# State space layer of a two-layer perceiver: where three of VectorE's scans stand among its other work

## The chip, the cores and the metric

One Trainium2 chip, of which the program uses one core. The metric is the time of one execution on the device in microseconds (us), lower is better. The kernel before took 2918.82 us, the median of three runs between 2916.55 and 2922.04 us.

## What is computed

The reference is two layers over 128 sequences of 32 tokens with 256 features: cross attention, a state space layer and a quantized feed-forward network, then a second cross attention, self attention and a mixture of experts. The change touches the state space layer alone:

```python
xz = jnp.einsum('btd,ed->bte', x, W_in)
xc, z = jnp.split(xz, 2, axis=-1)
xs = silu(conv3(xc, conv_w))
x_dbl = jnp.einsum('btd,ed->bte', xs, W_x)        # dt_param (64), Bp (16), Cp (16)
dt = softplus(dt_param @ W_dt.T + b_dt) + 1e-05
A_disc = jnp.exp(-jnp.exp(A_log)[None, None] * dt[..., None])
Bx = Bp[:, :, None, :] * dt[..., None] * xs[..., None]
s = A_t * s + Bx_t                                 # over the 32 tokens, 16 states a feature
y = C * s.sum(-1) + D_param * xs
x = x + jnp.einsum('btd,ed->bte', y, W_out) * silu(z)
```

## The kernel before

The layer is the function `state_space`. The 4096 tokens are cut into 16 tiles of 256 tokens (`NST`), and a software pipeline walks them: step n of the loop `for n in STEPS` works on tile n in its scans and on its neighbours from n - 2 to n + 4 in the parts that stand before and behind them. Every engine has an order of its own, written out by hand in its own copy of this loop, and takes its instructions strictly in that order; semaphores alone tie the engines together.

A tile has eight scans, four for each half of the features. Scan s of tile n (`scan`, L1917, one instruction of 128 x 1024 elements) reads its factors `A` and its drive, which TensorE has put into `psD[s % 2]`. There are only two such buffers. TensorE's `drive(n, s)` (L1744) therefore waits until the scan two before it has ended, and runs two scans ahead of VectorE in its own order:

```python
wait(pe, scan_done, at - 1)                  # drive(n, s): scan (n, s - 2) has ended
real(drive, n + (s + 2) // SLOTS, (s + 2) % SLOTS)   # ahead(n, s)
```

VectorE's order of a step is: scans 0 and 1, `lo_uT` (the low half of the turned inputs u, L1900, which waits for ScalarE's `hi_uT`, L1847), scan 2, `lo_xn` (L1890), scan 3, `read_out` of the tile before (L1923 and L1926; it waits until TensorE's `state_sum`, L1756, has summed all states of that tile), `lo_pb` (L1894), scans 4 and 5, `count` (L166), scan 6, `aggregate` (L170), `step_size` (L1908, which waits for ScalarE's softplus), `gate` of the tile before (L1933, which waits for TensorE's `out`), scan 7.

TensorE's order of a step is: drive 2, `turn_u` (L1730), the second quarter of the state sums, drive 3, `xnT` (L1676), the third quarter, drive 4, `dbl`, the fourth quarter, drive 5, a quarter of `conv`, drive 6, `dt_c` (it waits for `lo_pb`), a quarter of `conv`, drive 7, `out` (it waits for GpSimd's `split_y`), a quarter of `conv`, drive 0 of the next tile, the last quarter of `conv`, drive 1 of the next tile, `z`, and the first quarter of the next state sum. That one writes `psS`, which `read_out`, `out` and `gate` share, and so waits for the gate:

```python
if h == 0:
    wait(pe, o_done, n)                      # state_sum(n, 0, first)
```

GpSimd's order of a step is: `halve` of the tile before (L1628, it waits for scan 7), `split_xs`, `halve` (scan 1), `ln`, `halve` (scan 3), `split_y` (the read-out's result), half of `spread_b`, `halve` (scan 5), the other half of `spread_b`, `drive` (u, from `step_size`), and `residual` (L1640), which waits for the gate. ScalarE's `decay` (L1856) fills the factors, 32 instructions a step, with the other work between them.

Of the kernel before, what the change touches and what calls it, by code (L numbers as in the profile page):

```python
# [34 lines left out]
def wait(eng, sem, value):  # L35

    if isinstance(value, int) and value <= 0:
        return
    eng.wait_ge(sem, value)
# [1480 lines left out]
def state_space(nc, d, xres, con, norm, spent):  # L1520
# [11 lines left out]
    with ExitStack() as ctx:  # L1532
# [46 lines left out]
        def real(f, n, *more):  # L1579

            if 0 <= n < NST:
                f(n, *more)

        def flat(t):
            return t[:].rearrange("p c t -> p (c t)")

        @block.sync
        def _(sync):
            sp.clear_spent(sync)
            for t, k in ((a_log, "A_log"), (b_dt, "b_dt"), (d_par, "D_param")):  # L1590
                sync.dma_start(t[:], d[pre + k]).then_inc(const_in, 16)
            sync.dma_start(own_t[:], d["m0_own_t"]).then_inc(const_in, 16)
# [288 lines left out]
        @block.vector  # L1881
        def _(dve):
            dve.wait_ge(rate_exp, 1)
            dve.tensor_scalar(rate[:], rate[:], -1.0, None, ALU.mult).then_inc(const_ready, 1)
            dve.tensor_scalar(d_par[:], d_par[:], YS, None, ALU.mult).then_inc(const_ready, 1)
            dve.wait_ge(const_ready, 2)

            def lo_xn(n):
                dve.wait_ge(xn_hi, n + 1)
                dve.tensor_tensor(flat(xnp[1]), psX[:], flat(xnp[0]), ALU.subtract).then_inc(xn_lo, 1)  # L1890

            def lo_pb(n):
                dve.wait_ge(pb_hi, n + 1)
                dve.scalar_tensor_tensor(PB[1][:], psP[0:96, 0:ST], 1.0 / WS, PB[0][:], ALU.mult, ALU.subtract)  # L1894
                dve.tensor_tensor(Bt[1][:].rearrange("p t n -> p (t n)"), psP[:, ST:ST + 2 * NS],
                                  Bt[0][:].rearrange("p t n -> p (t n)"), ALU.subtract).then_inc(pb_lo, 1)

            def lo_uT(n):
                dve.wait_ge(uT_hi, n + 1)
                dve.scalar_tensor_tensor(flat(uT[n % 2][1]), psP[:], US, flat(uT[n % 2][0]), ALU.mult, ALU.subtract)\  # L1900
                    .then_inc(uT_lo, 1)

            def step_size(n):
                dve.wait_ge(sp_relu, n + 1)
                dve.wait_ge(sp_log, n + 1)
                wait(dve, a_done, 2 * (n - 1))
                wait(dve, u_done, n - 1)
                dve.scalar_tensor_tensor(flat(dt[n % 2]), psZ[:], 1e-5, sp_a[:], ALU.add, ALU.add).then_inc(dt_done, 1)  # L1908

            def scan(n, s):  # L1910
                k, jp, at = 2 * n + s // 4, s % 4, SLOTS * n + s
                if jp == 0:
                    dve.wait_ge(a_done, k + 1)
                    wait(dve, s_mm, k - 2)
                dve.wait_ge(drive_mm, at + 1)
                states, rates = (t[k % 3][:, 2 * jp:2 * jp + 2].rearrange("p j n t -> p (j n t)") for t in (S, A))
                dve.tensor_tensor_scan(states, rates, psD[at % 2][:], 0.0, ALU.mult, ALU.add).then_inc(scan_done, 1)  # L1917

            def read_out(n):
                dve.wait_ge(s_mm, 2 * n + 2)  # L1920
                dve.wait_ge(c_done, n + 1)
                wait(dve, yp_lo, n)
                dve.tensor_tensor(psS[:], Cm[n % 4][:], psS[:], ALU.mult).then_inc(y_prod, 1)  # L1923
                dve.wait_ge(y_prod, n + 1)
                for h in range(C):
                    last = dve.scalar_tensor_tensor(y[:, h, :], xs[n % 4][:, h * ST:(h + 1) * ST], d_par[:, h:h + 1],  # L1926
                                                    psS[:, h * ST:(h + 1) * ST], ALU.mult, ALU.add)
                last.then_inc(y_done, 1)

            def gate(n):  # L1930
                dve.wait_ge(o_mm, n + 1)
                wait(dve, x_done, n)
                dve.scalar_tensor_tensor(o[:], psS[:], 1.0 / (YS * WS), zs[n % 4][:], ALU.mult, ALU.mult).then_inc(o_done, 1)  # L1933

            def count(n):
                dve.wait_ge(x_done, n + 1)
                for g in (2 * n, 2 * n + 1):
                    statistics.count(dve, g)

            def aggregate(n):  # L1940
                for g in (2 * n, 2 * n + 1):
                    statistics.aggregate(dve, g)

            for n in STEPS:
                real(scan, n, 0)
                real(scan, n, 1)
                real(lo_uT, n + 1)
                real(scan, n, 2)
                real(lo_xn, n + 3)
                real(scan, n, 3)  # L1950
                real(read_out, n - 1)
                real(lo_pb, n + 2)
                real(scan, n, 4)
                real(scan, n, 5)
                real(count, n - 2)
                real(scan, n, 6)
                real(aggregate, n - 2)
                real(step_size, n + 2)
                real(gate, n - 1)
                real(scan, n, 7)  # L1960
            count(NST - 1)
            aggregate(NST - 1)

# [1067 lines left out]
```

## Time and profile before

| what | value |
|---|---|
| median of three runs | 2918.82 us |
| the profiled execution's own time | 2914.7 us |
| its span, first to last instruction | 2912.8 us |
| TensorE, busy | 2513.5 us, 86% of the span |
| VectorE, busy | 2056.3 us, 71% |
| ScalarE, busy | 1769.7 us, 61% |
| GpSimd, busy | 1557.9 us, 53% |
| mean granted TensorE clock | 0.926 of full speed |
| scans of the state space layer | 128, from 943.9 to 1396.4 us |

A busy share says how long an engine had an instruction in work, not how long it was the one that the others waited for. Matmuls overlap and their ends are modelled, so starts are better measured than lengths: where a length of TensorE's work is wanted, the distance from one start to the next is taken. The timeline merges neighbouring instructions of one form into one row, with their number at the end (x3), and in brackets stands how long the engine was idle before the row and who ended the idle time.

### The profile page before, as it was taken

To read this page: it belongs to the slowest core of one execution; us is meant where nothing else is said; L and a number is where in the kernel's file an instruction comes from. 1 tells how busy PE (TensorE), PEld (TensorE's weight loads), DVE (VectorE), ACT (ScalarE), POOL (GpSimd) and SP (SyncE) were. 2 spreads that over 40 slices of the span, in tenths; PEclk is the share of its full clock that TensorE was granted. 3 is DMA by queue.
4 is the path that set the end of the run, shared out by engine and by line. 5 is a ranking of instruction groups with operands and counts; after the bars stand their busy time and mean duration, and the time that the engine had idled before them with its cause. 6 is when DMAs were issued, how large, how long until landed. Compare 5 with 4: busy or idle time off the path is not lost. (4 is left out here: it accounts for less than half of the span.)

```text
span 2912.8 us, 77437 instructions
## 1 busy us (share of the span) xinstructions
PE 2513.5 (86%) x30042; PEld 1986.0 (68%) x30042; DVE 2056.3 (71%) x4606; ACT 1769.7 (61%) x4139; POOL 1557.9 (53%) x1602
## 2 busy tenths in 40 slices
PE   3999999999995898988597999999995888651998
PEld 2887788887873555554255888888884666551998
DVE  4778788788773778787344777777775888662554
ACT  2777777777774867775144666666663666443443
POOL 3656566556544777775103556556552677405443
PEclk9999999999996889998698999999997999855999
DMA  4222222222200000000001121111110000156664
GB/s 136 67 67 67 67 56 56 67 67 67 67 9 21 1 1 1 1 1 1 31 1 61 60 60 59 47 60 60 47 45 18 2 2 2 36 209 218 237 237 153
DMA packets 122999, 179.42 MB, mean 62 GB/s; under 512 B 10128, under 2 KB 106064, under 8 KB 120464
## 3 DMA queue, kind: packets, MB, share of 16 engines
q1 hardware_dynamic: 117968, 159.91, 17.9%
q0 software_dynamic: 4672, 14.57, 1.4%
q8 instruction: 244, 4.00, 0.6%
q14 instruction: 115, 0.94, 0.1%
HBM read 118.99 MB, written 14.56 MB: 46 GB/s over the span
## 5 line engine op out<-in xcount | busy, mean ns | idle before, releaser
L601 ACT ACTIVATE x_prob<-x_prob,x_nm 128x257 f32<-128x257 f32 x512 | 254.5, 499 | 176.6 <-DVE x_nm L689 176.6
L1917 DVE TENSOR_TENSOR_SCAN m_s<-m_a,m_psD 128x1024 f32<-128x1024 f32 x128 | 286.2, 2269 | 2.3 <-PE m_psD L1744 2.3
L1201 DVE SCALAR_TENSOR_TENSOR x_pTl<-x_psS,x_pTh 128x1024 f16<-128x1024 f32 x128 | 156.8, 1225 | 123.8 <-ACT x_pTh L1122 123.8
L689 DVE CUSTOM_DVE_ANT_0 x_prob<-x_psS,x_masked,x_lastv 128x256 f32<-128x256 f32 x512 | 217.3, 481 | 24.5 <-PE x_psS L513 20.6
L1856 ACT ACTIVATE m_a<-m_dt,m_rate 128x248 f32<-128x248 f32 x512 | 206.8, 492 | 0.0
L908 POOL TENSOR_TENSOR x_qbdh<-x_qh,all_mask4h 128x1024 f16<-128x1024 f16 x32 | 60.6, 1893 | 239.8 <-PE x_psV L948 236.3
L1628 POOL TENSOR_TENSOR m_s<-m_s 128x1024 f32<-128x1024 f32 x64 | 150.5, 2352 | 68.0 <-DVE m_s L1917 68.0
L1135 ACT ACTIVATE x_vh<-x_psV 128x512 f16<-128x512 f32 x128 | 76.4, 597 | 161.1 <-PE x_psV L948 161.1
L898 POOL TENSOR_SCALAR x_ctxh<-x_ctx 128x512 f16<-128x512 f32 x128 | 78.8, 616 | 163.4 <-DMA x_ctx<-in_ctxT 163.4
L418 PE MATMUL x_psK<-x_ctxh,x_wkh 128*128 128x256 f16 x512 | 141.2, 276 | 27.8 <-DVE x_kl L702 23.3
L2833 ACT ACTIVATE e1t_g<-e1t_psH,e1t_bias 128x128 f32<-128x128 f32 x312 | 88.9, 368 | 114.2 <-PE e1t_psH L2781 114.2
L900 POOL TENSOR_TENSOR x_ctxl<-x_ctx,x_ctxh 128x512 f16<-128x512 f32 x128 | 149.5, 1168 | 10.7
L352 POOL TENSOR_TENSOR x_ctxl<-x_ctx,x_ctxh 128x512 f16<-128x512 f32 x128 | 148.2, 1157 | 10.7
L948 PE MATMUL x_psK<-x_ctxh,x_wkh 128*128 128x256 f16 x512 | 141.2, 276 | 3.1 <-POOL x_ctxl L900 2.3
L1116 ACT ACTIVATE x_psS<-x_psS 128x1024 f32<-128x1024 f32 x128 | 129.2, 1009 | 24.1 <-PE x_psS L1045 24.1
L418 PE MATMUL x_psK<-x_ctxh,x_wkl 128*128 128x256 f16 x512 | 141.4, 276 | 0.0
L418 PE MATMUL x_psK<-x_ctxl,x_wkh 128*128 128x256 f16 x512 | 141.4, 276 | 0.0
L948 PE MATMUL x_psV<-x_wvh,x_ctxh 128*128 128x256 f16 x512 | 141.1, 276 | 0.0
L418 PE MATMUL x_psV<-x_wvh,x_ctxh 128*128 128x256 f16 x512 | 140.0, 274 | 0.0
L948 PE MATMUL x_psK<-x_ctxl,x_wkh 128*128 128x256 f16 x512 | 140.0, 273 | 0.0
L948 PE MATMUL x_psK<-x_ctxh,x_wkl 128*128 128x256 f16 x512 | 140.0, 273 | 0.0
L418 PE MATMUL x_psV<-x_wvl,x_ctxh 128*128 128x256 f16 x512 | 140.0, 273 | 0.0
(555 smaller groups left out, 10211.2 us busy)
## 6 DMA issues: line engine op xcount, KB each, us to landing
x_ctx<-in_ctxT SPq DMA_DIRECT2D x64, 1024.0 KB, 5.8
all_xres<-e_wh SPq DMA_DIRECT2D x39, 512.0 KB
all_xres<-e_wl SPq DMA_DIRECT2D x39, 512.0 KB
x_mraw<-in_mask SPq DMA_DIRECT2D x128, 128.5 KB, 6.0
e1r_stage<-in_L_ffn_w SPq DMA_DIRECT2D x16, 1024.0 KB, 5.2
e_rows<-e1r_pad POOLq DMA_DIRECT2D x1, 5070.0 KB, 25.0
e1t_row<-e_rows SPq DMA_DIRECT2D x39, 130.0 KB
all_xres<-in_x SPq DMA_DIRECT2D x4, 1024.0 KB, 9.8
```

What stands on the lines that cost most here:

```text
L352: pool.tensor_tensor(lo[:, j], src, hi[:, j], ALU.subtract).then_inc(ctx_split, 1)
L418: last = pe.matmul(out, a, b, start=m == 0, stop=m == len(prods) - 1)
L601: last = act.activation(prob[b % NP][:, s, :], prob[b % NP][:, s, :], ACT.Exp, bias=nm[b % NP][:, s:s + 1], scale=-1.0, accum_out=sm[b // ...
L689: dve.tensor_tensor_reduce(prob[b % NP][:, s, 0:LAST], psS[:, s * LAST:(s + 1) * LAST], masked[g % 2][:, j, :], -SC, lastv[g % 2][:, j, s: ...
L900: pool.tensor_tensor(lo[:, j], src, hi[:, j], ALU.subtract).then_inc(ctx_split, 1)
L948: last = pe.matmul(out, a, b, start=m == 0, stop=m == len(prods) - 1)
L1116: act.activation(psS[c % 2][:], psS[c % 2][:], ACT.Sigmoid, scale=SC).then_inc(sig_done, 1)
L1201: dve.scalar_tensor_tensor(pT[c % 4][1][:].rearrange("p r k n -> p (r k n)"), psS[c % 2][:], PS, pT[c % 4][0][:].rearrange("p r k n -> p ( ...
L1628: pool.tensor_tensor(lower, lower, upper, ALU.add).then_inc(half_done, 1)
L1856: last = act.activation(A[k % 3][:, :, m, 1:T], dt[n % 2][:, h, :].rearrange("p (j t) -> p j t", t=T)[:, :, 1:T], ACT.Exp, scale=rate[:, h ...
L1917: dve.tensor_tensor_scan(states, rates, psD[at % 2][:], 0.0, ALU.mult, ALU.add).then_inc(scan_done, 1)
L2833: act.activation(g[c % 2][:, k, :], psH[c % 2 * 2 + k // 4][:, k % 4 * P:(k % 4 + 1) * P], ACT.Gelu_apprx_tanh, scale=1.0 / WS, bias=bias[ ...
```

## The change

Three of VectorE's eight scans move up in its order by one place or more. Scan 2 moves ahead of `lo_uT`, scan 3 ahead of `lo_xn`, scan 4 ahead of `read_out` and `lo_pb`, and scan 7 ahead of `gate`. No instruction is added or taken away, no wait is changed, and the orders of the other engines stay. Seen from the scans, `lo_uT`, `lo_xn`, `read_out`, `lo_pb` and `gate` each come one scan later.

```diff
                 real(scan, n, 0)
                 real(scan, n, 1)
+                real(scan, n, 2)
                 real(lo_uT, n + 1)
-                real(scan, n, 2)
+                real(scan, n, 3)
                 real(lo_xn, n + 3)
-                real(scan, n, 3)
+                real(scan, n, 4)
                 real(read_out, n - 1)
                 real(lo_pb, n + 2)
-                real(scan, n, 4)
                 real(scan, n, 5)
                 real(count, n - 2)
                 real(scan, n, 6)
                 real(aggregate, n - 2)
                 real(step_size, n + 2)
+                real(scan, n, 7)
                 real(gate, n - 1)
-                real(scan, n, 7)
```

## Rows read from the trace of the kernel before

**Rows 1.** Windows: length, busy PE PEld DVE ACT POOL (x), granted clock, DMA share, GB/s
```profile
973.35:1319.68 346.33, 314.94 (x2137) 201.23 (x2136) 274.78 (x248) 252.47 (x565) 259.68 (x191) 0.91 0.00 1
1319.68:1348.31 28.63, 22.89 (x127) 13.17 (x127) 22.74 (x21) 18.95 (x44) 18.95 (x14) 0.82 0.00 1
1348.31:1375.09 26.78, 20.69 (x97) 10.75 (x97) 21.21 (x17) 13.14 (x33) 13.16 (x8) 0.75 0.00 1
1375.09:1413.00 37.91, 26.10 (x117) 16.57 (x116) 20.21 (x25) 0.00 (x0) 14.72 (x10) 0.77 0.00 0
```

**Rows 2.** Waits from 973.35 to 1319.68 us: who for whom, total us, times, longest
```profile
PE m_psD L1744 <- DVE m_s L1917: 31.1, 21, 2.5
DVE m_psS L1923 <- PE m_psS L1756: 22.4, 12, 1.9
DVE m_o L1933 <- PE m_psS L1665: 22.1, 12, 3.6
```

**Rows 3.** VectorE's timeline, one step: start us, length us, instruction, [idle before <- releaser]
```profile
1120.47 0.69 DVE L1900 SCALAR_TENSOR_TENSOR m_ut1l<-m_psP,m_ut1h 128x512 f16<-128x512 f32 x1 [1.67 <-ACT m_ut1h L1847]
1121.08 2.28 DVE L1917 TENSOR_TENSOR_SCAN m_s<-m_a,m_psD 128x1024 f32<-128x1024 f32 x1
1123.54 0.69 DVE L1890 TENSOR_TENSOR m_xnl<-m_psX,m_xnh 128x512 f16<-128x512 f32 x1 [0.18 <-ACT m_xnh L1806]
1124.14 2.28 DVE L1917 TENSOR_TENSOR_SCAN m_s<-m_a,m_psD 128x1024 f32<-128x1024 f32 x1
1128.29 0.70 DVE L1923 TENSOR_TENSOR m_psS<-m_c,m_psS 128x512 f32<-128x512 f32 x1 [1.87 <-PE m_psS L1756]
...
1130.24 4.45 DVE L1917 TENSOR_TENSOR_SCAN m_s<-m_a,m_psD 128x1024 f32<-128x1024 f32 x2
...
1135.26 2.26 DVE L1917 TENSOR_TENSOR_SCAN m_s<-m_a,m_psD 128x1024 f32<-128x1024 f32 x1
...
1138.19 0.69 DVE L1908 SCALAR_TENSOR_TENSOR m_dt<-m_psZ,m_sp_a 128x512 f32<-128x512 f32 x1 [0.53 <-issue]
1141.21 0.69 DVE L1933 SCALAR_TENSOR_TENSOR m_o<-m_psS,m_zs 128x512 f32<-128x512 f32 x1 [2.33 <-PE m_psS L1665]
1141.82 6.63 DVE L1917 TENSOR_TENSOR_SCAN m_s<-m_a,m_psD 128x1024 f32<-128x1024 f32 x3
```

**Rows 4.** TensorE's timeline, same step: drives 2 to 6, a `conv`, `out`, drives 1 and 2
```profile
1118.40 0.39 PE L1744 MATMUL m_psD<-m_bd0h,m_ut0h 32*128 32x512 f16 x2
...
1121.46 0.39 PE L1744 MATMUL m_psD<-m_bd0h,m_ut0h 32*128 32x512 f16 x2
...
1124.53 0.39 PE L1744 MATMUL m_psD<-m_bd0h,m_ut0h 32*128 32x512 f16 x2
...
1128.18 0.39 PE L1744 MATMUL m_psD<-m_bd0h,m_ut0h 32*128 32x512 f16 x2
...
1128.93 0.28 PE L1665 MATMUL m_psX<-m_xnh,m_wt1h 128*128 128x256 f16 x1
...
1132.57 0.39 PE L1744 MATMUL m_psD<-m_bd0h,m_ut0h 32*128 32x512 f16 x2 [2.48 <-DVE m_s L1917]
...
1139.69 0.28 PE L1665 MATMUL m_psS<-m_wouth,m_yh 128*128 128x256 f16 x1
...
1144.15 0.39 PE L1744 MATMUL m_psD<-m_bd1h,m_ut1h 32*128 32x512 f16 x2 [0.15 <-DVE m_s L1917]
...
1148.05 0.39 PE L1744 MATMUL m_psD<-m_bd1h,m_ut1h 32*128 32x512 f16 x2
```

**Rows 5.** TensorE alone in windows of 2 us, same step: length, busy us, granted clock
```profile
1130.00:1132.00 2.00, 0.09 (x1) 1.00 0.00 0
1134.00:1136.00 2.00, 2.00 (x11) 0.50 0.03 8
```

**Rows 6.** ScalarE's timeline, same step: the last decays before softplus, and its start
```profile
1126.88 4.81 ACT L1856 ACTIVATE m_a<-m_dt,m_rate 128x248 f32<-128x248 f32 x12
1135.20 0.84 ACT L1829 ACTIVATE m_sp_a<-m_psZ,m_b_dt 128x256 f32<-128x256 f32 x2 [3.52 <-PE m_psZ L1665]
```

## The prediction

> **What bounds the kernel now.** I read the windows first, then the waits of the longest window, then the timelines of one step on VectorE, TensorE and ScalarE. The windows are cut where TensorE starts drive 2 of tiles 1, 13, 14 and 15 (the last runs to the end of the layer). The window from 973.35 to 1319.68 us holds 12 whole steps of 28.86 us each (346.33 / 12) [rows 1]. In it TensorE is busy for 314.94 us, 91% of the time, VectorE for 22.9 us a step (274.78 / 12), GpSimd for 21.6 and ScalarE for 21.0. No engine is full, so waits between them matter. TensorE's matmuls wait for VectorE's scans for 31.1 us in all, 2.6 us a step, and the longest wait is 2.5 us [rows 2]: it is one place, once a step.
>
> The timelines show the place. All times below are offsets from T, the start of drive 2 of the step at 1118.40 us; its next start, 1148.05, makes that step 29.65 us long [rows 4]. Drive 6 needs scan 4. VectorE stands idle for 1.87 us ahead of the read-out, which starts at T+9.9 when TensorE has finished the state sums, then does `read_out` and `lo_pb`, and starts scan 4 only at T+11.84 [rows 3]. TensorE is at drive 6 at T+11.7 (1132.57 less 2.48) but starts it at T+14.17 [rows 4]. So VectorE first waits for TensorE with a scan in its hands whose drive is already there, and TensorE then waits for that scan. A second price follows. The granted clock is 1.00 in the window in which TensorE stands still and 0.50 right behind it, the lower of its two levels (1.2 instead of 2.4 GHz) [rows 5]. Over the 12 steps the clock is 0.91 [rows 1], so 0.09 x 346.3 = 31 us, another 2.6 us a step, is lost to it.
>
> **The change part by part.** Nothing is added or removed; each of the eight scans, and each moved step, has the length that it has now. Only starts move. No instruction issues a DMA, and no DMA queue is passed: the DMA share of the stage is 0.00 [rows 1].
>
> Scan 2 ahead of `lo_uT`. Scan 1 ends at T+0.4 (scans 7, 0 and 1 end at 1141.82 + 6.63 = 1148.45, the next T is 1148.05 [rows 3, 4]) and `lo_uT` waits 1.67 us for ScalarE [rows 3]. A drive takes 0.75 us (1128.18 to 1128.93 [rows 4]), so scan 2 is ready at T+0.75 and fills that wait. `lo_uT` comes some 2 us later against T. Who waits for it: `dbl`, which writes the same `psP` and starts at T+6.9, behind drive 4 (T+6.13), and drive 0 of the next tile at T+18. Both have slack; cost 0.
>
> Scan 3 ahead of `lo_xn`. Drive 3 starts at T+3.06 [rows 4]. `lo_xn` slips to about T+6.2; its first reader is `conv` at T+10.5 (1128.93) [rows 4]. Cost 0.
>
> Scan 4 ahead of `read_out` and `lo_pb`. This is the part that pays. Drive 4 is done at T+6.9 (6.13 + 0.75), so scan 4 runs from T+6.95 to T+9.2. The state sums end at T+9.9 as now, so the read-out still starts there and `split_y` and `out` behind it lose nothing. Scan 4 is over 2.5 us before TensorE reaches drive 6 at T+11.7: the 2.48 us wait goes, and I take the clock's fall with it. From drive 6 to `out` TensorE took 7.12 us (1132.57 to 1139.69), nearly all of it at half clock [rows 4, 5]. It holds two drives and 21 matmuls (12 of `dt_c`, 9 of `conv`). At full clock, `out`, a `conv`, a drive and a `conv` (30 matmuls and a drive) take 4.31 us (1139.69 to 1144.00), which is (4.31 - 0.75) / 30 = 0.12 us a matmul, so the middle costs 21 x 0.12 + 2 x 0.75 = 4.0 us: 3.1 us less. What is late next: `dt_c` needs `lo_pb`, which still ends at T+11.84, before drive 6 is over at T+12.4. Drive 7 needs scan 5: from T+11.85 to T+14.1, while TensorE is there at T+14.9.
>
> Scan 7 ahead of `gate`. VectorE waits 2.33 us for `out` in this step and 22.1 us in 12 steps [rows 2, 3]. Scan 6 now runs from T+14.7 to T+16.9, and `step_size` to T+17.65 if softplus is there. ScalarE ends its decays at T+13.3 (1126.88 + 4.81) and its softplus takes 3 us (1135.20 to `step_size` at 1138.19), so T+16.3 [rows 3, 6]: in time by 0.7 us. Scan 7 runs to T+19.9. Drive 1 of the next tile, which needs it, is reached at T+20.0 (11.7, 4.0 for the middle and 4.3 from `out` on [rows 4]). These are so near to each other that I allow for a wait of 0 to 0.3 us where there were 0.15. The gate, queued behind, ends at T+20.5. Behind it on VectorE are scans 0 and 1, on GpSimd `residual` and the halving of scan 7, and on TensorE the first quarter of the state sums, which starts at most 2.3 us ahead of the next drive 2 (drives 2 and 3 are 3.06 apart, with a drive, `turn_u` and such a quarter between their starts [rows 4]), so not before T+21.7. Cover 1.2 us; cost 0.
>
> The new step: 29.65 - 2.48 - 3.1 = 24.0 (24.1 with the little wait at its longest). The mean comes out alike: 28.86 - 2.6 - 2.6 = 23.7, and the waits that stay. VectorE's 22.9 us fit into 24.0 with 1.1 to spare, so TensorE sets the pace with hardly a pause. I take 24.0. Saved: 12 x 4.85 = 58 us.
>
> Outside the 12 steps: steps 13 and 14 take 28.63 and 26.78 us with VectorE busy for 22.74 and 21.21 and the clock at 0.82 and 0.75 [rows 1]. They can't fall below VectorE's work, so they give at most 5.9 and 5.6; TensorE has less to do there and will still wait here and there, so I take 5 and 4 (bounds 2 and 5.7 each). The last window starts with a step of the same kind, but there the halving of scan 7 stands behind the `residual` that waits for the gate, so I take 1 (0 to 3). Tile 0's step has no read-out; I take 1 (0 to 2.4, the steady wait). Sum: 58 + 11 = 69 us.
>
> One rule of the Trainium skill speaks against the term for the clock. First the row: a wait of 0.15 us stands ahead of drive 1 and the half clock is seen behind the 2.48 us wait only [rows 4, 5]. The page "TensorE: Matmul & The Clock Gate", section "A second HAM failure mode: psum-queue depth-cycling", says that micro-idles between groups of matmuls can be enough for the clock to swing between its levels. By the row the clock term is worth its 2.6 us a step, by the rule nothing; the rule's case is the first rival.
>
> **The rivals.** (A) The clock still falls once a step, on the short wait ahead of drive 1 or by itself. For it: the wait there may grow to 0.35 us. Against: behind today's 0.15 us wait, drive 1, `z` and a quarter of the sums take 3.9 us (1144.15 to 1148.05), which is what they cost at full clock (0.75, 12 x 0.12 and at most 2.3). It leaves the wait's 2.6 us x 12 = 31 us and about 5 in the other steps: 36 us saved, 2883 us.
>
> (B) GpSimd becomes the bound. It has 21.6 us of work in a step of 24.0, and `residual`, waiting for a later gate, now stands ahead of the halving of scan 7. For it: it waits for other engines in several places of its order, and each such wait comes off the 2.4 us that are left. Against: the gate ends only 0.6 us behind scan 7, and what `halve` hands on is read a step later, by the third quarter of the sums. If its pace or a lock-step with the gate makes the step 25.2, 12 x 1.2 = 14 us less is saved: 55 us, 2864 us. [...]
>
> (C) Slower. Place: VectorE's queue ahead of scan 7. Scan 7 and the gate both stand behind `step_size`, which waits for ScalarE's softplus; the gate frees `psS` for the next state sum. If softplus came 2.5 us or more behind T+17, TensorE would stand still at drive 1 and fall to half clock in the state sums behind it, From 2.5 us on the stall and the 3.1 us of clock together are more than the 4.85 saved; with a wait of 5 us they are 8.1, and 12 x (8.1 - 4.85) = 39 us more than now, about 2958 us. Against: ScalarE stood idle for 3.52 us ahead of softplus [rows 6], so the order of its work leaves it in time.
>
> (D) No change. The order moves but another chain holds the step at 28.9 us, for which I find no row; 2919 us.
>
> **How the numbers follow.** The sum is made against the profiled execution, 2914.7 us, which is 4.1 below the median of the runs, 2918.8. 2914.7 - 69 = 2845.7; against the median 2849.8. I predict 2850 us. Chances: forecast 0.70 (its own range 2840 to 2862), A 0.12, B 0.12, C 0.04, D 0.02. The range from 2841 to 2883 takes in B and A and the lower bound of the last steps; some 0.15 is left out. A measurement of this kernel tells 0.2%, some 6 us, from no change. Faster 0.94, same 0.02, slower 0.04.
>
> **What would show it.** In the profile after: no wait of 2.5 us ahead of L1744 in drive 6; a granted clock of 0.98 or more from about 975 to 1265 us; `lo_uT` to `lo_uT` 24.0 us; VectorE's waits ahead of `lo_uT` and the gate gone, that ahead of the read-out down from 1.87 to about 0.7 us; the next layer starting some 69 us earlier and taking as long as now. Wrong would be: a clock near 0.9 with the wait gone (A), idle time on GpSimd at zero (B), long waits ahead of L1908 (C).

## The result and the profile after

The changed kernel takes 2842.27 us in the median (2838.36 to 2851.27, four runs) against 2917.96 us of the kernel before on the same chip (2916.55 to 2922.04, four runs). The ratio is 0.9754, with a 95% interval of 0.9733 to 0.9775. By the medians that is 75.7 us less, by the ratio 72 us (66 to 78), where 69 had been forecast (2850 us, range 2841 to 2883). The median stands only 1.3 us above the lower end of that range, and two of the four runs (2838.36 and 2838.47) lie below it. Two executions of the changed kernel, beside the last pair of experiments, took 5722.71 and 7934.94 us; they are left out of every median here, and what made them slow is open. The profiled execution took 2838.4 us, its span 2836.4 us, 76.4 less than before.

Four scans move in the diff, scans 2, 3, 4 and 7; the three of the title and of the text on the change are a miscount.

First the windows, cut as in [rows 1], where drive 2 of tiles 1, 13, 14 and 15 starts (length, then the busy times of PE, PEld, DVE, ACT and POOL, the granted clock, the DMA share, GB/s), of the changed kernel:

```profile
970.22:1255.77 285.55, 284.88 (x2137) 189.52 (x2136) 272.41 (x249) 251.98 (x565) 256.50 (x190) 1.00 0.01 1
1255.77:1279.10 23.33, 20.09 (x128) 11.88 (x128) 22.12 (x21) 18.84 (x44) 19.20 (x15) 0.88 0.00 1
1279.10:1302.59 23.49, 19.79 (x99) 10.47 (x98) 22.28 (x18) 13.14 (x33) 13.34 (x9) 0.79 0.00 1
```

The same 12 steps now take 285.55 us, 23.80 each, where they took 346.33, or 28.86 each (means: the first of the changed kernel's 12 takes 23.68, the others 23.81). TensorE is busy for 284.88 of them, and its granted clock is 1.00 instead of 0.91. The work of VectorE, ScalarE and GpSimd in them has hardly changed (272.4, 252.0 and 256.5 us): nothing was made faster, the same work has been packed.

All waits of VectorE in the same window, the counterpart of [rows 2]; TensorE's matmuls have none there that the view shows:

```profile
DVE m_s L1917 <- PE m_psD L1744: 6.6, 26, 0.5
DVE m_psS L1923 <- PE m_psS L1756: 6.1, 12, 0.5
```

VectorE waited for 22.4 us ahead of the read-out and 22.1 us ahead of the gate; now it waits 6.1 us and none. Short waits for a drive, at most 0.5 us, are new.

VectorE's timeline of one step, the counterpart of [rows 3]. Here T is 1089.13 us:

```profile
1092.22 0.66 DVE L1900 SCALAR_TENSOR_TENSOR m_ut1l<-m_psP,m_ut1h 128x512 f16<-128x512 f32 x1
1093.06 2.29 DVE L1917 TENSOR_TENSOR_SCAN m_s<-m_a,m_psD 128x1024 f32<-128x1024 f32 x1 [0.17 <-PE m_psD L1744]
1095.26 0.67 DVE L1890 TENSOR_TENSOR m_xnl<-m_psX,m_xnh 128x512 f16<-128x512 f32 x1
1096.22 2.29 DVE L1917 TENSOR_TENSOR_SCAN m_s<-m_a,m_psD 128x1024 f32<-128x1024 f32 x1 [0.29 <-PE m_psD L1744]
1099.02 0.70 DVE L1923 TENSOR_TENSOR m_psS<-m_c,m_psS 128x512 f32<-128x512 f32 x1 [0.51 <-PE m_psS L1756]
...
1106.13 0.65 DVE L1908 SCALAR_TENSOR_TENSOR m_dt<-m_psZ,m_sp_a 128x512 f32<-128x512 f32 x1
1106.71 2.27 DVE L1917 TENSOR_TENSOR_SCAN m_s<-m_a,m_psD 128x1024 f32<-128x1024 f32 x1
1108.90 0.66 DVE L1933 SCALAR_TENSOR_TENSOR m_o<-m_psS,m_zs 128x512 f32<-128x512 f32 x1
1109.48 6.63 DVE L1917 TENSOR_TENSOR_SCAN m_s<-m_a,m_psD 128x1024 f32<-128x1024 f32 x3
```

The read-out starts at T+9.9 (1099.02), where it started before, but scan 4 (1096.22) stands ahead of it now and ends at T+9.4. The second scan of the last row begins right behind the first: the gate delays nobody.

TensorE's timeline of the same step, the counterpart of [rows 4]: drives 5 and 6, `out`, drive 1 and drive 2.

```profile
1098.91 0.39 PE L1744 MATMUL m_psD<-m_bd0h,m_ut0h 32*128 32x512 f16 x2
...
1100.76 0.39 PE L1744 MATMUL m_psD<-m_bd0h,m_ut0h 32*128 32x512 f16 x2
...
1104.66 0.28 PE L1665 MATMUL m_psS<-m_wouth,m_yh 128*128 128x256 f16 x1
...
1109.04 0.39 PE L1744 MATMUL m_psD<-m_bd1h,m_ut1h 32*128 32x512 f16 x2
...
1112.93 0.39 PE L1744 MATMUL m_psD<-m_bd1h,m_ut1h 32*128 32x512 f16 x2
```

Drive 6 starts at T+11.6 with no wait ahead of it that the view shows, and the stretch from there to `out` takes 3.90 us instead of 7.12. From `out` to drive 1 it is 4.38 us (4.46 before), from drive 1 to drive 2 3.89 (3.90 before).

Where the 76.4 us of the span come from, part by part (T is the start of drive 2):

| stretch | before, us | after, us | less |
|---|---|---|---|
| before the first scan | 943.88 | 943.06 | 0.8 |
| first scan to T of tile 1 | 29.47 | 27.16 | 2.3 |
| 12 steady steps | 346.33 | 285.55 | 60.8 |
| step 13 | 28.63 | 23.33 | 5.3 |
| step 14 | 26.78 | 23.49 | 3.3 |
| T of tile 15 to the last gate | 35.15 | 33.52 | 1.6 |
| behind the last gate | 1502.56 | 1500.29 | 2.3 |

The first and the last row, 3.1 us together, lie outside of the loop that was changed.

The small rows of this table are those of one execution. The changed kernel was profiled twice more, beside later experiments, and both times the 12 steps were the same (285.56 and 285.60 us), but the stretches around them were not. The first stretch took 32.15 us, 2.7 more than in the kernel before; step 13 took 24.2, step 14 20.7 and the last stretch 31.1. Only their sum holds: from the first scan to the last gate it is 393.05, 393.65 and 393.7 us, against 466.36 before, 73 us less. What lies behind the last gate differs by some 8 us between the three executions (1500 to 1508 us).

### The profile page after: what moved, and what is told of

The parts are those of the page before. It is cut to its first block and busy times, and to the rows that moved or that the text cites. A ratio compares the mean times of both kernels' runs of the same rounds, so it can differ in the third digit from the quotient of the medians.

```text
span 2836.4 us, 77437 instructions
## 1 busy us (share of the span) xinstructions
PE 2475.5 (87%) x30042; PEld 1968.4 (69%) x30042; DVE 2052.7 (72%) x4606; ACT 1769.3 (62%) x4139; POOL 1556.7 (55%) x1602
## 5 line engine op out<-in xcount | busy, mean ns | idle before, releaser
L1917 DVE TENSOR_TENSOR_SCAN m_s<-m_a,m_psD 128x1024 f32<-128x1024 f32 x128 | 288.3, 2271 | 12.5 <-PE m_psD L1744 12.5
L1135 ACT ACTIVATE x_vh<-x_psV 128x512 f16<-128x512 f32 x128 | 76.4, 597 | 160.4 <-PE x_psV L948 160.4
L418 PE MATMUL x_psK<-x_ctxl,x_wkh 128*128 128x256 f16 x512 | 141.4, 276 | 0.0
L418 PE MATMUL x_psK<-x_ctxh,x_wkl 128*128 128x256 f16 x512 | 141.4, 276 | 0.0
L539 PE MATMUL x_psO<-x_pT,x_v 128*64 128x128 f32 x2048 | 139.9, 279 | 0.0
L418 PE MATMUL x_psV<-x_wvh,x_ctxl 128*128 128x256 f16 x512 | 139.9, 273 | 0.0
```

Source lines behind the costliest of these rows:

```text
L418: last = pe.matmul(out, a, b, start=m == 0, stop=m == len(prods) - 1)
L539: last = pe.matmul(psO[64 * r:64 * r + 64, to:to + P], V[b % NV][:, kt, c * P + 64 * r:c * P + 64 * r + 64], pT[b % NW][:, kt, s * P:(s + ...
```

## The experiments

All times are medians beside runs of the kernel before on the same chip. The steps come from each kernel's own profile, from drive 2 to drive 2. In the orders that have scan 4 ahead of the read-out they repeat to within 0.02 us, all but the first of the 12, which is up to 0.8 us shorter; the step that is quoted is that of the others. Orders are given as VectorE's step, with s0 to s7 for the scans.

**Only scan 4 moved.**

```diff
                 real(lo_xn, n + 3)
                 real(scan, n, 3)
+                real(scan, n, 4)
                 real(read_out, n - 1)
                 real(lo_pb, n + 2)
-                real(scan, n, 4)
                 real(scan, n, 5)
```

> Only scan 4 is moved (ahead of the read-out); scans 2, 3 and 7 stay where they were before. Theory (the gain comes from scan 4, because it ends TensorE's wait ahead of drive 6 and the fall of the clock with it): the wait and the half clock are gone, but VectorE's wait of 1.7 us for lo_uT stays and pushes scan 7 to the end at T+20.7 against 19.8, so TensorE waits some 0.9 us ahead of drive 1: step 24.7 us, about 2853 us. Rival (the four moves each bring a share of their own, by the waits on VectorE that each fills): 1.87 of the 6.2 us of VectorE's waits filled, step about 27 us, about 2895 us.

Measured: 2856.3 us against 2912.7, ratio 0.9799 (0.9769 to 0.9829); steady step 24.61 us. The window of the 12 steps, and TensorE's only wait in it:

```profile
975.03:1269.65 294.62, 284.97 (x2137) 189.60 (x2137) 271.53 (x248) 251.38 (x565) 257.13 (x189) 1.00 0.00 1
```

```profile
PE m_psD L1744 <- DVE m_s L1917: 9.5, 11, 0.9
```

By the windows, one move out of four brings 4.31 of the 5.06 us of a step ((346.33 - 294.62) / 12), with the clock at 1.00. The rival of equal shares falls. What is left is the forecast wait of 0.9 us ahead of drive 1.

**All but scan 4** (s0 s1 s2 `lo_uT` s3 `lo_xn` `read_out` `lo_pb` s4 s5 `count` s6 `aggregate` `step_size` s7 `gate`).

```diff
                 real(scan, n, 3)
                 real(lo_xn, n + 3)
-                real(scan, n, 4)
                 real(read_out, n - 1)
                 real(lo_pb, n + 2)
+                real(scan, n, 4)
                 real(scan, n, 5)
```

> Scans 2, 3 and 7 are moved, scan 4 stays behind the read-out and lo_pb. Theory: drive 6 waits 2.5 us as before and half clock follows; only the 0.15 us ahead of drive 1 can go, 2 us in all: 2916 us, the same as before within the noise. Rival (each move brings its share): VectorE's waits of 1.7 and 2.0 us a step filled, step about 25 us, about 2872 us.

Measured: 2904.0 us against 2912.7, ratio 0.9970 (0.9956 to 0.9983). TensorE's waits in the 12 steps, and the window:

```profile
PE m_psD L1744 <- DVE m_s L1917: 29.7, 12, 2.5
```

```profile
969.70:1315.33 345.63, 315.92 (x2137) 202.16 (x2137) 276.00 (x249) 252.55 (x565) 258.97 (x191) 0.91 0.00 1
```

In the steady steps it is as the theory has it: 345.63 us against 346.33, the wait of 2.5 us twelve times, the clock at 0.91. VectorE no longer waits ahead of `lo_uT` and hardly for the gate (0.8 us in all), and that is worth hardly anything there. But the kernel is 9 us faster than before where 2 were expected. That is a miss, and most of it lies in the last steps: step 13 takes 24.62 us instead of 28.63, step 14 24.63 instead of 26.78. Before, TensorE stood still for 2.18 us ahead of drive 1 of tile 14, behind a gate that waited for `out`; with scan 7 ahead of the gate it does not.

**Only scan 7 moved.**

```diff
                 real(step_size, n + 2)
+                real(scan, n, 7)
                 real(gate, n - 1)
-                real(scan, n, 7)
```

> Only scan 7 is moved (ahead of the gate). Theory: TensorE does not wait for scan 7 by more than 0.15 us now, so the step shortens by 0.15 us at most: 2916 us, same. Rival: VectorE's 22.1 us of waiting for the gate's input are given back: 2897 us.

Measured in a single run: 2902.6 us beside a median of 2912.7. That is 10 us less where about 3 were expected, nearer to the rival's 2897 than to the theory, so the windows have to decide. The 12 steps take 343.65 us (346.33 before), step 13 24.73 and step 14 24.43. TensorE's waits in step 13, and those of the kernel before:

```profile
PE m_psD L1744 <- DVE m_s L1917: 3.6, 1, 3.6
```

```profile
PE m_psD L1744 <- DVE m_s L1917: 5.7, 2, 3.6
```

The second wait of the kernel before is gone, and this move alone accounts for the gain of the run above. In the steady steps VectorE's waiting for `out` fell from 22.1 to 0.4 us, and the 12 steps are only 2.7 us shorter: nearly all of it was slack. What it gives is seen at drive 1, which now starts 1.84 us behind drive 0 instead of 2.06.

**The kernel before, with TensorE's standing still filled.** VectorE's order is that of before; TensorE is given work whose result is overwritten.

```diff
+            def filler(n, count):
+                pe.wait_ge(zs_done, n + 1)
+                for m in range(count):
+                    pe.matmul(psZ[:, 0:ST], Wt[0][0][:, 0, 0:P], xnp[0][:, 0, :], start=True, stop=True)
...
                 real(conv, n + 3, 0, 0)
+                real(filler, n + 2, 20)
                 ahead(n, 4)
```

> The kernel before, VectorE's order unchanged; TensorE does 20 more matmuls of 256 columns (2.2 us at full clock, their result is overwritten) in each step just ahead of drive 6, where it stood still. This separates the two prices: the time of standing still stays, the clock's fall should go if standing still is its cause. Theory: granted clock 1.00 through the steady steps, step 28.9 - 2.6 = 26.3 us, about 2885 us, although TensorE has more to do. Rival (the clock falls once a step by itself or by load): the clock stays at 0.91 and the step is 28.9 us or longer, 2918 us or more.

Measured: 2885.8 us against 2912.7, ratio 0.9909 (0.9876 to 0.9941); step 26.58 us. The window, and two rows of TensorE's timeline, the filler and drive 6 behind it:

```profile
974.20:1293.09 318.89, 312.01 (x2378) 213.15 (x2378) 273.33 (x249) 252.59 (x565) 258.87 (x191) 1.00 0.00 1
```

```profile
1118.52 2.35 PE L1776 MATMUL m_psZ<-m_xnh,m_wt0h 128*128 128x256 f16 x20
1121.16 0.39 PE L1744 MATMUL m_psD<-m_bd0h,m_ut0h 32*128 32x512 f16 x2 [0.29 <-DVE m_s L1923]
```

With some 240 useless matmuls more (2378 - 2137) the 12 steps are 27 us shorter, and the granted clock is 1.00. So the fall of the clock was caused by the standing still and not by load, and by the means of the steps the two prices can be told apart: 28.86 - 26.58 = 2.28 us a step for the clock, and 26.58 - 23.80 = 2.78 us for the wait itself and what little else the new order gives.

**The changed kernel again**, the yardstick for the three kernels below.

> The changed kernel once more, on the chip of this call, as the yardstick for the kernels beside it: about 2842 us, step 23.8 us.

Measured: 2841.9 us against 2917.1, ratio 0.9734 (0.9704 to 0.9765); step 23.81 us.

**All but scan 7**, the changed kernel with scan 7 put back behind the gate.

```diff
                 real(step_size, n + 2)
-                real(scan, n, 7)
                 real(gate, n - 1)
+                real(scan, n, 7)
```

> The changed kernel with scan 7 put back behind the gate. Theory (each stretch of VectorE between the read-out and scan 7 is now on TensorE's path): the gate's 0.6 us stand ahead of scan 7, which ends at T+20.4 instead of 19.8; TensorE waits 0.65 us ahead of drive 1 instead of 0.05: step 24.4 us, 7 us more than the changed kernel, about 2849 us. Rival (the move of scan 7 is worth nothing, as it is alone): 2842 us, step 23.8 us.

Measured: 2851.2 us, ratio 0.9765 (0.9733 to 0.9796); step 24.41 us. TensorE's waits in the 12 steps:

```profile
PE m_psD L1744 <- DVE m_s L1917: 7.4, 12, 0.7
```

The step is 0.60 us longer, which is the gate's length, and TensorE's wait is 7.4 / 12 = 0.62 us. The intervals of the two ratios overlap; the steps tell the kernels apart, the times alone do not. The move of scan 7 is worth 0.2 us a step at most by itself (343.65 against 346.33 in the run above; where scans 2 and 3 moved too it was 345.63, with the same 1.84 us from drive 0 to drive 1 and more of the long half-clock steps) and 0.6 us once scan 4 is ahead of the read-out.

**More work for TensorE**, the changed kernel with 9 matmuls of the filler above a step.

> The changed kernel with 9 more matmuls of 256 columns a step on TensorE ahead of drive 6 (1.0 us, their result is overwritten). Theory (TensorE sets the pace): step 24.75 us, 12 to 13 us more, about 2854 us. Rival (VectorE sets it, with TensorE only following): up to 1 us a step is absorbed, 2842 us.

Measured: 2847.1 us beside the yardstick's 2841.9; step 24.67 us, 0.86 more. So nearly all of the 0.99 us of added work is paid (drive 5 to drive 6 takes 2.83 instead of 1.84 us), and 0.13 is taken in: drive 1 starts 1.84 us behind drive 0, in the changed kernel 1.97. TensorE's own work is 23.68 us a step, and 0.13 us of waiting for scan 7 comes on top, too short for the view of waits. The whole moved by only 5 us where 12 were expected. The 12 steps account for 10.4 us (296.00 against 285.56), and the stretches ahead of them and behind them were 3.7 us shorter in this execution than in the yardstick's (from the first scan to the last gate 400.4 against 393.65 us, 6.8 more); the rest is within the spread of the runs, 9 us for the yardstick.

**More work for VectorE, in two places**, the changed kernel with two statistics instructions a step that write to a spare tile: between scans 5 and 6 in the first kernel, between `lo_uT` and scan 3 in the second.

```diff
+            def repeat(n):
+                dve.wait_ge(x_done, n + 1)
+                for t in range(2):
+                    dve.bn_stats(spare[:, t, :], xres[:, (2 * n + t) * D:(2 * n + t + 1) * D])
...
                 real(count, n - 2)
+                real(repeat, n - 2)
                 real(scan, n, 6)
```

```diff
                 real(lo_uT, n + 1)
+                real(repeat, n - 3)
                 real(scan, n, 3)
```

> The changed kernel with 0.65 us more work a step on VectorE (two statistics instructions written to a spare tile), between scans 5 and 6. Theory (VectorE has about 1 us to spare over a whole step, but none between the read-out and scan 7): scan 7 ends 0.65 us later and TensorE waits for it, step 24.4 us, about 2850 us. Rival (VectorE's spare time takes it in): 2842 us.

> The changed kernel with the same 0.65 us more work a step on VectorE, this time between lo_uT and scan 3, ahead of the place where VectorE waits for the state sums. Theory: scans 3 and 4 come up to 0.5 us later, the waits of 0.17, 0.29 and 0.51 us behind them shrink by as much, the read-out starts when it did: step 23.8 us, 2842 us as the changed kernel. Rival (any VectorE work is on the path): 8 us more, 2850 us.

Measured: 2851.6 us ahead of scan 6, step 24.46; 2840.7 us ahead of scan 3, step 23.81. The two ran on different chips, so it is the steps that compare. TensorE's waits of the first, VectorE's of the second, each in its 12 steps:

```profile
PE m_psD L1745 <- DVE m_s L1918: 7.8, 11, 0.7
```

```profile
DVE m_psS L1924 <- PE m_psS L1757: 6.1, 12, 0.5
DVE m_s L1918 <- PE m_psD L1745: 1.9, 6, 0.5
```

The same 0.65 us cost 0.65 us in one place and nothing in the other. In the second kernel VectorE's waits for a drive fell from 6.6 to 1.9 us and took the work in. The stretch of VectorE from the read-out to scan 7 has no slack; the stretch ahead of the read-out has.

**A step further**: `lo_pb` ahead of the read-out, and the gate ahead of scan 7 in the last tile's step alone.

```diff
                 real(scan, n, 4)
-                real(read_out, n - 1)
                 real(lo_pb, n + 2)
+                real(read_out, n - 1)
...
+                if n == NST - 1:
+                    gate(n - 1)
                 real(scan, n, 7)
-                real(gate, n - 1)
+                if n != NST - 1:
+                    real(gate, n - 1)
```

> The changed kernel with lo_pb ahead of the read-out in every step, and the gate ahead of scan 7 in the last tile's step alone. Theory: lo_pb fits into the 0.5 us for which VectorE waits ahead of the read-out, the steady step stays at 23.8 us; in step 13 TensorE's wait of 1.35 us for lo_pb ahead of dt_c goes, and in the last step the state sums start up to 1 us earlier: 1 to 3 us less than the changed kernel, 2840 us, hardly to be told from it by time but by its windows. Rival (the read-out slips, and split_y and out behind it): step above 23.8 us.

Measured: 2835.2 us against 2913.6, ratio 0.9744 (0.9722 to 0.9767). It ran a second time, beside the changed kernel:

> The changed kernel as the yardstick for the kernel beside it, on the same chip: 2842 us, step 23.81 us.

> The kernel with lo_pb ahead of the read-out and the last gate ahead of the last scan 7 once more, beside the changed kernel. By its windows the steady step was 23.68 against 23.81 us, so 12 x 0.13 = 1.6 us, and some us in the last three steps. Theory: 3 to 6 us less than the changed kernel in the medians. Rival: what was gained in the last steps was the phase of the clock in one execution; 1 to 2 us less, not to be told apart.

Measured: the changed kernel 2841.9 us in the four runs that count (0.9744, 0.9724 to 0.9765), this one 2839.2 us (0.9746, 0.9725 to 0.9766), both against 2914.0. The windows of the 12 steps, the changed kernel's first:

```profile
974.11:1259.71 285.60, 284.90 (x2138) 189.56 (x2138) 272.06 (x248) 251.47 (x565) 256.08 (x189) 1.00 0.01 1
```

```profile
971.19:1255.35 284.16, 284.16 (x2137) 189.60 (x2136) 273.30 (x248) 251.19 (x564) 254.95 (x189) 1.00 0.01 1
```

The steady step is 23.68 instead of 23.81 us, and TensorE is busy for the whole of its window. From T of tile 1 to the last gate it is 359.4 against 361.5 us, 2.2 less. The medians differ by 2.7 us, the ratios by nothing: by time the two can't be told apart, which is the rival's case and not the theory's 3 to 6 us. Its gain of some 2 us rests on the windows alone. The 0.13 us of a step stand at one place. These are drives 0 and 1 of one step, of the changed kernel (of the run with the table above) and of this one:

```profile
1107.07 0.39 PE L1744 MATMUL m_psD<-m_bd1h,m_ut1h 32*128 32x512 f16 x2
1109.04 0.39 PE L1744 MATMUL m_psD<-m_bd1h,m_ut1h 32*128 32x512 f16 x2
```

```profile
1107.54 0.39 PE L1744 MATMUL m_psD<-m_bd1h,m_ut1h 32*128 32x512 f16 x2
1109.38 0.39 PE L1744 MATMUL m_psD<-m_bd1h,m_ut1h 32*128 32x512 f16 x2
```

In the changed kernel scan 7 ends at 1108.98, 0.06 us ahead of drive 1, and in this one at 1109.03, 0.35 us ahead of it: with `lo_pb` done while VectorE would wait for the state sums, its work behind the read-out is shorter, and TensorE no longer waits for scan 7.

## Why the prediction was right

The place and both prices were right. The wait ahead of drive 6 and the half clock behind it are gone in the steady steps; moving scan 4 alone brings 4.31 us a step, and putting it alone back takes all but 0.06 us a step away again (345.63 / 12 = 28.80).

- The new step: forecast 24.0 us, measured 23.80. From drive 6 to `out` 4.0 us were forecast and 3.90 measured; the wait ahead of drive 1 was put at 0 to 0.3 us and is 0.13 (1.97 us from drive 0 to drive 1, against 1.84 in the kernels where scan 7 is early). The row of TensorE's waits was read too simply: its 21 waits are 12 of 2.48 us and 9 of 0.15, two places and not one, though the sum used both. The subtraction gives 24.07, not 24.0. VectorE's wait ahead of the read-out was put at about 0.7 us and is 0.51.
- The two terms of the mean: I split the 5.2 us a step into 2.6 for the wait and 2.6 for the clock. By the filled kernel the clock cost 2.28 and the wait with the rest 2.78. The clock's term was 0.3 too large. A part of that can be seen: in the filled kernel, at full clock, TensorE waits up to 0.29 us ahead of drive 1, where it waited 0.15 before [rows 4], so some of what half clock lost it would have waited for VectorE anyway. The rest is not told apart. The step of 29.65 us that was read for the sum is not typical : seven of the 12 steps take 28.1 us, four 29.6 to 29.7 and one 31.1, so the 3.1 us of clock hold for that step, and the mean is below.
- The steps outside: in the profiled pair step 13 gave 5.3 us (5 forecast), step 14 3.3 (4), the last stretch 1.6 (1), the start 2.3 (1), 12.5 in all for 11. That the parts agree so well is luck: in the two later profiles of the changed kernel step 13 gives 4.4 us, step 14 6.1, the last stretch 4.1, and the start takes 2.7 us more than before. Their sum, some 12, is what held. The reason for step 13 was only half told. In the kernel before it has two waits, and scan 7's move removes the one ahead of drive 1, for some 4 us of its own (24.73 instead of 28.63). I had costed that move at nothing but the 0.15 us of the steady step.
- The missing 6.7 us of the sum (75.7 instead of 69): 60.8 - 58.2 = 2.6 in the steady steps, 1.5 in the stretches around them, and 3.1 in the profiled pair outside of the layer, which no step of the prediction had; 0.7 lies between the profiled pair's 76.4 and the medians' 75.7. The runs of the two kernels spread by 5.5 and 12.9 us, so all but the first part is within the spread. Had the median come out 1.4 us lower, by chance alone, it would have left the range, though the step was forecast to within 0.2 us: the lower end was too near to the forecast.
- Rival A, a clock that falls on short waits: it did not come in the steady steps. The changed kernel has hardly a wait left there, and the windows of the two kernels that wait once a step ahead of drive 1, 0.6 us without scan 7's move and 0.9 us with scan 4's alone, have a granted clock of 1.00 too. At both ends of the loop the clock did fall behind waits far shorter than 2.48 us, where several stand close together (the last section has the rows). The Trainium skill, page "TensorE: Matmul & The Clock Gate", section "A second HAM failure mode: psum-queue depth-cycling", says that micro-idles between groups of matmuls can be enough; these places agree with it, and in the steady steps it did not decide.
- Rival B, GpSimd as the bound: it is busy for 256.5 of 285.6 us and waits for 2.0 us a step ahead of `split_y`. It did not decide.
- Rival C, a late softplus: `step_size` starts at 1106.13 right behind `aggregate`, without a wait. But the two kernels with 0.6 us more ahead of scan 7 show how near it was: the step grew by 0.60 and 0.65 us, by all that VectorE was late.

## What to carry to other kernels

Where two engines hand each other work through two buffers, look at what stands in one queue ahead of the instruction that the other engine waits for. A wait whose own input comes late (the read-out at T+9.9) should not stand ahead of an instruction whose input is long there (scan 4), and the gain is counted at the waiting engine, not by the idle time of the one that is reordered: here 22 us of VectorE's waiting ahead of the gate were worth 3 us in the steady steps, and one wait of 1.9 us a step, filled with scan 4, was worth 4.3 us a step. Price a pause of TensorE with what its clock loses behind it, and several short ones close together like a long one; where the pause can't be removed, filling it is worth a trial.

## What the hardware showed that was not expected

- A pause of 2.5 us cost almost as much again in the matmuls behind it (2.28 us a step), and 2.2 us of useless matmuls in the pause gave all of it back. Pauses of 0.6 and 0.9 us once a step left the granted clock at 1.00 in the whole window.
- But short waits close together do bring the clock down. At the start of the loop TensorE's drives wait for scans several times in a row, with little work between them. These are the rows of the changed kernel's second profile, and TensorE alone in windows of 2 us around them:

```profile
944.24 0.39 PE L1744 MATMUL m_psD<-m_bd0h,m_ut0h 32*128 32x512 f16 x2 [0.35 <-DVE m_s L1917]
946.42 0.39 PE L1744 MATMUL m_psD<-m_bd0h,m_ut0h 32*128 32x512 f16 x2 [0.77 <-DVE m_s L1917]
948.60 0.39 PE L1744 MATMUL m_psD<-m_bd0h,m_ut0h 32*128 32x512 f16 x2 [0.77 <-DVE m_s L1917]
```

```profile
946.00:948.00 2.00, 1.41 (x10) 1.00 0.00 0
950.00:952.00 2.00, 2.00 (x22) 0.50 0.00 0
```

The clock stays at 0.50 until about 973 us there; in the first profile, with waits of 0.63, 0.77, 0.77 and 0.88 us, it is at 0.50 only from about 953 to 963, and the longer half clock goes with the longer first stretch, 32.15 against 27.16 us. In step 13 it fell behind waits of 1.35 and 0.71 us, which end 2.2 us apart.
- The price of the same pause was not constant. With one and the same order of work the steady steps of the kernel before took 28.1, 29.6 or 31.1 us. The pause was 2.48 us in each, and the length of the half clock behind it made all but some 0.2 us of the difference. Without the pause the steps repeat to 0.02 us. What sets that length is open; no run here tells.
- A wait can be too short for the view of waits and still be in every step. The 0.13 us ahead of drive 1 appear in no row of waits; they are seen only in the distance from start to start, 1.97 us in the changed kernel and 1.84 where scan 7 is over earlier.
